# A new order for the first block of an attention and feed-forward kernel

## What is computed

```
x = x + L0_xattn(layernorm(x), ctx)   # q, k, v; 16 heads of 16; softmax over 64 keys; then relu(out @ W1 + b1) @ W2 + b2
x = x + L0_ffn(layernorm(x))          # gate: top 2 of 8 experts; relu(x @ wi + bi + lora of the expert) @ wo, gated
x = x + L1_xattn(layernorm(x), ctx)   # one head of 256, softmax over 64 keys
x = x + L1_ffn(layernorm(x))          # x @ weight.T + pooled(x) @ disha
```

## Time and profile before

| | |
|---|---|
| runs of the kernel | median 313.52 us, 313.37 to 314.22, 3 runs |
| the profiled execution | 313.58 us, span 311.6 us: 1.98 us lie around the span |
| PE busy | 296.1 us, 95% of the span |
| PEld busy | 273.4 us, 88% |
| DVE busy | 257.1 us, 83% |
| ACT busy | 172.1 us, 55% |
| POOL busy | 161.2 us, 52% |

### The profile page before, as it was taken

One profiled execution on the slowest core, in us unless ns is written; L12 is line 12 of the kernel. 1 busy time (PEld: TensorE's weight loads), 2 busy tenths in 40 slices (PEclk: granted clock), 3 DMA queues, 4 the chain that ended last, 5 costly groups with the idle time before them and its releaser, 6 DMA issues.

```text
span 311.6 us, 6575 instructions
## 1 busy us (share of the span) xinstructions
PE 296.1 (95%) x2488; PEld 273.4 (88%) x2488; DVE 257.1 (83%) x706; ACT 172.1 (55%) x359; POOL 161.2 (52%) x156
## 2 busy tenths in 40 slices
PE   6879998999999999999999999999999999999982
PEld 5749887999989998999999998999899998999971
DVE  3689878979899988998799889998899879756676
ACT  3447488675567357535846465835853584434521
POOL 2754666695085705581386308560559044803562
PEclk9799999999999999999999999999999999999996
DMA  7993230015021230133012311122023000000000
GB/s 227 394 375 110 61 78 2 0 36 135 2 17 38 68 102 2 17 96 112 2 17 69 102 37 17 44 76 87 3 27 94 34 2 0 2 23 13 0 36 34
DMA packets 15903, 20.17 MB, mean 65 GB/s; under 512 B 2912, under 2 KB 11872, under 8 KB 15616
## 3 DMA queue, kind: packets, MB, share of 16 engines
q1 hardware_dynamic: 14176, 16.18, 18.9%
q10 hardware_dynamic: 1696, 3.57, 3.2%
...
## 4 chain that ended last, share of the span: by engine, by line
PE 63%; DVE 24%; ACT 5%; POOL 3%; issue 2%; DMA 2%; SPq 0%; DVEq 0%; POOLq 0%
PE psI L338 12%; PE psI L552 12%; PE psP L347 8%; PE psI L347 4%; PE psT L338 4%; DVE st L1254 3%; ACT xn L950 3%; DVE qu_l L1288 2%; DVE mx L1296 2%; PE psP L487 2%; DMA kv<-in_kv 2%; PE psS L347 2%; PE psS L460 2%; POOL rs L1726 2%; PE psT L362 2%
## 5 line engine op out<-in xcount | busy, mean ns | idle before, releaser
L1726 POOL TENSOR_TENSOR rs<-ve,mhalf 128x2 f32<-128x2 f32 x30 | 22.0, 732 | 88.7 <-DVE ve L1265 88.7
L1749 POOL TENSOR_TENSOR hid_l<-r,hid_h 128x512 fp32r<-128x512 f32 x32 | 40.9, 1290 | 16.1 <-ACT hid_h L1029 16.1
L552 PE MATMUL psI<-at_h,lb_h 128*128 128x256 f32 x120 | 34.8, 290 | 0.8 <-DVE at_l L1378 0.8
L552 PE MATMUL psI<-at_h,lb_l 128*128 128x256 f32 x120 | 33.9, 282 | 0.0
L552 PE MATMUL psI<-at_l,lb_h 128*128 128x256 f32 x120 | 33.7, 281 | 0.0
L1386 DVE SCALAR_TENSOR_TENSOR r<-psI,nbi,r 128x256 f32<-128x256 f32 x60 | 26.1, 476 | 6.5 <-PE psI L552 6.5
L1743 POOL TENSOR_TENSOR hs_l<-hs,hs_h 128x512 fp32r<-128x512 f32 x15 | 19.6, 1312 | 20.1 <-ACT hs_h L1009 19.5
L950 ACT ACTIVATE xn<-xmid,nmr,rs 128x256 f32<-128x256 f32 x16 | 8.7, 593 | 35.6 <-POOL nmr L1730 35.6
L1024 ACT ACTIVATE r<-psI,first 128x256 f32<-128x256 f32 x60 | 25.1, 473 | 4.4 <-PE psI L552 4.4
L552 PEld LDWEIGHTS psI<-at_h,lb_h 128*128 128x128 f32 x120 | 22.6, 188 | 4.3 <-ACT r L1024 2.9
L1029 ACT ACTIVATE hid_h<-r 128x512 fp32r<-128x512 f32 x32 | 20.0, 627 | 11.2 <-DVE r L1386 11.0
...
## 6 DMA issues: line engine op xcount, KB each, us to landing
stack<-qu_h SPq DMA_DIRECT2D x56, 64.0 KB, 2.1
...
stack<-qu_l SPq DMA_DIRECT2D x28, 64.0 KB, 2.1
...
raw_wo<-in_wo SPq DMA_DIRECT2D x1, 1024.0 KB, 13.2
```

Source lines behind the costliest of these rows:

```text
L552: last = mm(bank[:, k * T:(k + 1) * T], (WH, WL)[x]["lb"][:, 0, f * P:(f + 1) * P], AT[y][:, which, :], start=False, stop=q == 2, skip_gro ...
L1726: G_.tensor_tensor(rs[:, :], ve[:, :], mhalf[:, :], ALU.pow).then_inc(S(f"ln{j}_rs"), 1)
L1749: G_.tensor_tensor(HL[:, two, :], R1[:, two, :], as32(HH[:, two, :]), ALU.subtract).then_inc(S("hidl"), 1)
```

## The change

Nothing of what is computed changes; the first block's work is put in another order, and some of it on other engines.

- x of block 0 is loaded in two halves, one from SP and one from ACT, where the second stands ahead of ACT's other loads (a1, wq, w1, w2). kv1 is loaded ahead of wi.
- values of v0 for batch 0 no longer stand between keys0 and the transposes on PE; they and query_means come after a_queries(0). query_means works on fp32r operands (4 products) in place of fp32 ones.
- first_attend issues the sums for two pairs, then the values, in banks of their own, so that the reciprocal waits for the sums alone.
- Block 1's queries are computed in three passes placed around the two halves of a_out(0); values1 and folded_keys come earlier, and the row scores of block 1 after them.
- v0 is copied by ACT (value_rows) and masked by POOL (first_values) in place of DVE; the copy of the query means goes from DVE to ACT.
- Low parts: w1 and ga go from DVE to POOL, w2 from POOL to DVE; the first half of wo moves from the end of POOL's opening into body(1), behind `gated`. The second half of the indicators moves to the end of body(2).
- fold_turn moves behind a_scores of body(1), and f_lora_transposes(0) ahead of them; lora_high(0) goes ahead of the exps on ACT.
- Fillers: 4, then 2 after keys0, 1 before a_queries(0) (before: 4, then 2 and 1 around a_queries(0)).

The core of the diff:

```diff
@@ -44,7 +44,7 @@
...
+HIGH_ORDER = ["wq", "w1", "w2", "wi0", "ga", "wi1", "lb", "wo"]
 GW = 2 * KEYS + D
...
-                sp.dma_start(x_of_block(b), x_v[b]).then_inc(S("x_in"), 16)
+                if b == 0:
+                    sp.dma_start(XINS[0][:, 0, :], x_v[0][:, 0, :]).then_inc(S("x_in"), 16)
+                else:
+                    sp.dma_start(x_of_block(b), x_v[b]).then_inc(S("x_in"), 16)
...
-            sp.wait_ge(S("x_in"), 16)
+            sp.wait_ge(S("x_in"), 32)
             load_x(1)
+            sp.dma_start(kv1[:, :], io["kv1"]).then_inc(S("ld_kv1"), 16)
             load("wi")
             load("ga")
-            sp.dma_start(kv1[:, :], io["kv1"]).then_inc(S("ld_kv1"), 16)
...
+                    parts = [(P_(0)[:, m * T:(m + 1) * T], w("wq", m * P), x_of(XTA)) for m in range(KC)]
+                    last = passes(parts, range(KC), ((x, y),), (x, y) == (0, 0), y == 1)
+                    if y:
+                        last.then_inc(S("q_ps"), 1)
...
-                        last = mm(P_(m)[rows, T:2 * T], ones_pair, EX[:, c, :], start=True, stop=True)
+                        last = mm(FIRST_SUMS[m][rows, 0:T], ones_pair, EX[:, c, :], start=True, stop=True)
                 last.then_inc(S("pv"), 1)
+                if m == 0:
+                    pe.wait_ge(S("v0_ready"), 3)
+                for c in range(m * GPC, (m + 1) * GPC):
+                    rows = slice(PW * (c % GPC), PW * (c % GPC) + PW)
+                    last = mm(FIRST_VALUES[m][rows, 0:T], v0z[:, c * PW:(c + 1) * PW], EX[:, c, :], start=True, stop=True)
+                last.then_inc(S("pv"), 1)
...
                 if b == 0 and half == 0:
-                    pe.wait_ge(S("lo_wp"), 1)
+                    pe.wait_ge(S("lo_w"), 2)
+                    pe.wait_ge(S("ln1_l"), 2)
...
+                parts = [t["wq"][:, c * D:(c + 1) * D] for t in (wh, wl) for c in range(KC)]
                 for n, part in enumerate(parts):
-                    last = mm(S_(1)[:, 0:D], avg[:, 0:1].broadcast_to([P, P]), part, start=n == 0,
+                    last = mm(P_(1)[:, T:T + D], avg_r[:, :].broadcast_to([P, P]), part, start=n == 0,
...
-                if F_:
+                if F_ and f > 0:
                     f_lora_transposes(f)
                 if f == 0:
+                    fold_turn()
                     fold_means()
...
                 first_scores_less_maxima()
                 first_attend(0)
                 first_attend(1)
-                query_means()
-                transposes(1, 1, I_(0))
-                values(T_(1)[:, 0:D], kv0, 1).then_inc(S("v0_ps"), 1)
+                values(S_(1)[:, 0:D], kv0, 1).then_inc(S("v0_ps"), 1)
                 keys1()
+                pe.wait_ge(S("rec"), 1)
+                transposes(1, 1, P_(1))
+                values1()
                 a_hidden(0, 0)
-                pe.wait_ge(S("centred"), 2)
+                pe.wait_ge(S("v0"), BATCH)
                 a_hidden(0, 1)
-                a_queries(1, I_(1))
+                a_queries(1, ((0, 0),))
                 a_out(0, 0)
+                a_queries(1, ((1, 0),))
                 a_out(0, 1)
-                pe.wait_ge(S("kt1"), 1)
-                pe.wait_ge(S("v0"), BATCH)
-                a_row_scores(1, 0, T_)
-                a_row_scores(1, 1, S_)
-                values1()
+                a_queries(1, ((0, 1),))
                 folded_keys()
+                a_row_scores(1, 0)
+                a_row_scores(1, 1, I_)
+                pe.wait_ge(S("x1"), 1)
+                transposes(2, 0, P_(1))
                 pe.wait_ge(S("mx"), 2 * NT - 1)
-                transposes(2, 0, T_(1))
+                constant_parts()
+                f_gate(0, 1)
                 pe.wait_ge(S("mx"), 2 * NT)
-                constant_parts()
+                f_base(0, 0)
+                pe.wait_ge(S("ln2_l"), 1)
                 a_max_transposes(1)
-                f_gate(0, 1)
-                pe.wait_ge(S("gb"), 1)
-                f_base(0, 0)
                 constant_row()
-                pe.wait_ge(S("v1"), 1)
                 f_base(0, 1)
-                fold_turn()
+                f_lora_transposes(0)
...
+            def value_rows(b, bank):
+                act.wait_ge(S("v0_ps"), b + 1)
+                A(v0[:, b * D:(b + 1) * D], bank[:, 0:D], ACT.Identity).then_inc(S("v0"), 1)
...
+                if f == 0:
+                    act.wait_ge(S("kd_out0"), 32)
+                    act.wait_ge(S("kd_out1"), 32)
                     lora_high(f)
-                if A_:
-                    exps(a, 1)
+                exps(a, 0)
...
+            act.dma_start(XINS[0][:, 1, :], x_v[0][:, 1, :]).then_inc(S("x_in"), 16)
...
+                normalise(1, 0, x_of_block(0))
...
-                normalise(1, 0, x_of_block(0))
                 high(1, 0, XTA, T_(1))
                 high_weights("w1")
                 queries(0)
+                act.wait_ge(S("centred"), 1)
+                value_rows(0, P_(1))
+                A(wqm[:, :], P_(1)[:, T:T + D], ACT.Identity).then_inc(S("centred"), 1)
...
                 normalise(1, 1, x_of_block(1))
+                value_rows(1, S_(1))
                 attended(0, 0)
+                high(1, 1, XTA, P_(1))
                 high_weights("wi", 0, 2)
-                high(1, 1, XTA, I_(0))
                 attended(0, 1)
+                high_weights("ga")
                 high_weights("wi", 1, 2)
...
+                high_weights("wo")
                 maxima(1)
                 sorted_exps(0)
-                high_weights("wo")
...
             def first_attended(m):
-                dve.wait_ge(S("pv"), m + 1)
-                V.reciprocal(REC[:, m, :], P_(m)[:, T:2 * T]).then_inc(S("rec"), 1)
+                dve.wait_ge(S("pv"), 2 * m + 1)
+                V.reciprocal(REC[:, m, :], FIRST_SUMS[m][:, 0:T]).then_inc(S("rec"), 1)
                 dve.wait_ge(S("rec"), m + 1)
-                V.tensor_tensor(O32[:, m, :], P_(m)[:, 0:T], REC[:, m, :], MULT).then_inc(S("o32"), 1)
+                dve.wait_ge(S("pv"), 2 * m + 2)
+                V.tensor_tensor(O32[:, m, :], FIRST_VALUES[m][:, 0:T], REC[:, m, :], MULT).then_inc(S("o32"), 1)
...
                 first_attended(0)
                 first_attended(1)
-                dve.wait_ge(S("centred"), 1)
-                V.tensor_copy(wqm[:, :], S_(1)[:, 0:D]).then_inc(S("centred"), 1)
                 attended_low(0, 1)
-                low(1, 1, XTA, I_(0))
-                first_values(1, T_(1)[:, 0:D])
+                low_weights("w2")
+                low(1, 1, XTA, P_(1))
                 keys_of_second()
+                hidden_low(0, 1)
                 low_weights("wi", 1, 2)
-                hidden_low(0, 1)
-                queries_low(1)
-                low_weights("ga")
                 first_residual(0)
                 dve.wait_ge(S("x1"), 1)
                 norm_stats(2, 0, XMID)
-                row_max(1, 0, psT)
-                row_max(1, 1)
-                low(2, 0, XTF, T_(1))
+                queries_low(1)
...
+                    if f == 0:
+                        low_weights("wo", 0, 2)
...
+                if a == 2:
+                    pool.wait_ge(S("ln3_rs"), f + 1)
+                    indicators(1)
...
+            def first_values(b):
+                at = slice(b * D, (b + 1) * D)
+                ready = 3 * b
+                pool.wait_ge(S("v0"), b + 1)
+                G_.tensor_tensor(v0[:, at], v0[:, at], vmask, ALU.mult).then_inc(S("v0_ready"), 1)
+                pool.wait_ge(S("v0_ready"), ready + 1)
+                G_.tensor_tensor(v0[:, at], v0[:, at], bvrow0, ALU.add).then_inc(S("v0_ready"), 1)
+                if b == 0:
+                    pool.wait_ge(S("v0_ready"), 2)
+                    G_.tensor_tensor(v0z[:, :], v0[:, at], vmask, ALU.mult).then_inc(S("v0_ready"), 1)
...
-                pool.wait_ge(S("ld_first"), 16)
-                pool.wait_ge(S("ln1_nmr"), 1)
-                indicators(0)
-                indicators(1)
                 pool.wait_ge(S("ld_vrows"), 16)
                 G_.tensor_copy(heads[:, :], heads32).then_inc(S("tables"), 1)
-                low_weights("w2", 0, 1)
+                low_weights("w1", 0, 1)
+                first_values(0)
+                scale(1, 1)
+                pool.wait_ge(S("ld_first"), 16)
+                pool.wait_ge(S("ln1_nmr"), 2)
+                indicators(0)
+                second_row_keys()
+                attended_low(0, 0)
+                first_values(1)
                 pool.wait_ge(S("ld_kept"), 16)
                 residual(0)
-                scale(1, 1)
-                attended_low(0, 0)
-                pool.wait_ge(S("kt0_h"), KC)
-                second_row_keys()
+                low_weights("ga", 0, 1)
                 hidden_low(0, 0)
                 low_weights("wi", 0, 2)
```

142 lines of the change are left out of this document (63 added, 79 removed).

## The result

The changed kernel takes 317.61 us (median, 315.93 to 319.41) against 313.42 for the kernel before on the same chip; the ratio is 1.0138, 95% interval 1.0117 to 1.0159. The medians differ by 4.2 us, and the ratio stands for 4.3; 0.996 was forecast. The profiled execution took 318.99 us with a span of 316.0.

What follows compares the result with a forecast made beforehand. PE bounds the blocks behind the opening, so only the start of f_first counts: 0.2 us from xmid and 1.1 from the end make it 1.3 earlier, 313.58 to 312.3, median 312.2 us; range 310.5 to 314.5.

Steps and rivals of the forecast that it cites:

- Row scores of block 0: First stage of the opening: row scores start at 13.15 in place of 15.08, 1.9 us earlier, bounds 1.6 to 2.4.
- w1's landing: First stage: w1, behind half of x in ACT's queue, lands at 11.2 and sets w_h, qu_h and the row scores.
- The end part: From xmid to f_first: at_l no longer waits for gate, held by POOL's wo_l; 1.1 us gained.
- just in time: Block 1's query copies by SP: the stack DMAs land at 45.2, ahead of a_scores at 45.9.
- Rival (c): Ahead of xmid: POOL becomes the bound; 0.9 us slower, 314.5, if its wi_l starts later than 33.9; chance 0.15.
- (d): End of body(2): the moved indicators product ks holds up DVE; at most 2.81 us, about 1.4 net, 313.6; chance 0.04.
- The step that failed: Opening, on POOL: w_l of w1 (2.35 us) and three small v products end by about 16.8; values wanted at 19.
- The second failing step: First block's softmax chain: same instructions with PE at full clock ahead of it, so exps end 1.9 us earlier.
- Rival (b): Hole ahead of xn's transposes: PE's clock halves, f_first at 49.6, 0.4 later than before, 313.5 us; chance 0.25.
- The pivot: At xmid: POOL's wi_l goes before DVE's, so xmid comes at 35.05, 1.85 us behind x1_ps; PE hole 2.9 us.
- Rival (a): At xmid: DVE takes wi_l right behind hs_l, xmid at 33.2, f_first 1.8 us earlier, 311.6 us; chance 0.22.

Runs made afterwards that it cites:

- kb_wi: The changed kernel with POOL's w_l of w1 behind DVE's kd_l and POOL's half of wi_l behind DVE's half, no filler added; ratio 0.9943 to the kernel before.
- before_wo: The kernel before with only POOL's first half of wo_l moved from the end of its opening into body(1), behind gated; ratio 0.9936, median of all executions 313.98 us.
- warm: The changed kernel with six fillers on PE behind the first block's row scores; ratio 1.0054 to the kernel before.
- kb_free: The changed kernel with POOL's w_l of w1 made to wait until DVE's kd_l is done; ratio 1.0044 to the kernel before.
- kb_first: The changed kernel with DVE's kb ahead of xta_l, as in the kernel before, and nothing else; ratio 1.0061 to the kernel before.
- before_kv0: The kernel before with only batch 0's values of v0 moved behind the first block's queries, in their own bank, and fillers rearranged; 312.91 us, ratio 0.9975.
- kv0_wo: The kernel before with batch 0's values of v0 behind the first block's queries and wo_l's first half behind gated; 312.93 us, ratio 0.9988.
- best4: The changed kernel with POOL's w_l of w1 behind DVE's kd_l, POOL's wi_l half behind DVE's, four fillers behind the first row scores; 311.24 us, ratio 0.9901.

## Why the prediction was wrong

**The gains.** Row scores of block 0 were forecast at 13.15. In kb_wi they begin at 13.17 and the exps at 18.16, 1.9 earlier than before: this term was right in size, once DVE is free of POOL, though that is one execution against one, and the row scores of the kernel before stand at 15.08 in its profile and at 16.80 in before_wo's. Not right was its working, and the match is luck. x did land earlier (norm_stats at 3.70, not 4.60), but the half of x in ACT's queue put wq back (wq_h at 7.16, not 5.60 as before), so that xn, ready at 6.15, stood behind wq_h; w1's landing, which the prediction took for the limit, did not matter: in kb_wi w_h ran at 9.83, right behind xta_h, and the row scores came straight behind PE's own query_means (12.53 to 13.17), which the sum had as hidden. The end part was forecast at 1.1 and is worth 0.4 (xmid to f_first 13.53) to 1.0 (12.99 in warm). gate waits for nothing, as forecast (0.16 us at 51.86); but in the changed kernel a_scores of block 1 waits 0.42 us for the last stack DMA, which was "just in time" in the sum. Rival (c) did not happen: POOL's hs_l waited 1.79 us for ACT's hs_h, and its wi_l came directly behind it, so POOL was not the bound, though this product started at 36.03, past the 33.9 from which (c) has the kernel slower: it came late behind hs_h. Nor did (d): with ks in the body of block 2, f_first to the end is 262.2 us against 262.4.

**The step that failed** is in the part up to the first row scores: "POOL has w_l of w1 (2.35 ...) and three small v products ahead of the first values". It costed this product for POOL and for who waits for POOL, and not for DVE. The rule was known: in the next part the same text lets the engines get into each other's way, and counts 0.5 us there. But DVE's kb, 1.21 us with two SBUF inputs, was moved behind xta_l, a part of the diff that neither the list of changes nor the prediction names, and so it stood exactly where w_l starts. The price was 2.22 us up to the maxima.

**The second failing step** is "The softmax chain behind them (maxima, exps) is the same instruction for instruction, so the exps end 1.9 us earlier as well", with "PE at full clock, since two fillers now lie in the hole between keys and transposes" ahead of it. The instructions were the same, and row scores to exps took 6.53 us in place of 5.00. The fillers do lie there, and the clock was 1.00 there. But the kernel before had its half clock at 9.8 to 13.2 and was at 1.00 through the softmax; the changed one entered the softmax chain with a hole of 1.20 and then of 1.63 us and fell to 0.50 for the 10 us in which PE is the limit. Rival (b) looked for this only in the hole ahead of xn's transposes. The length of the hole does not decide it alone: with 0.85 us the clock fell in kb_wi and kb_free, with 0.86 it did not in the kernel before.

Measured against kb_wi and the kernels at full clock, the changed kernel's f_first is late by: 2.22 (kb and kd_l); 0.68 (maxima to exps: 3.87 from the start of the second maximum to the exps, 3.19 in kb_wi, whose clock fell only afterwards); 2.26 (exps to a_hidden, 10.11 against 7.84 or 7.85 in five kernels with the same instructions at 1.00); 1.88 (a_hidden to xmid, 9.07 against 7.19, POOL's wi_l); 0.41 (xmid to f_first, 13.53 against 13.12). That is 7.45 us, of which the change's own gains pay 2.9, and 4.5 remain. 4.1 are turns at the ports, 2.9 the clock, and 0.4 the wait for the stack DMA. The 2.9 gained are against the profiled execution of the kernel before, which had its half clock and a late kv0.

**The pivot** was right in kind and partly in place. The prediction gave it 1.85 us at DVE's wi_l; kb_first shows it there, the changed kernel on hs_l one instruction earlier, for 1.62 us of PE. With PE held there, the hole ahead of the transposes was 1.16 us in the changed kernel and not 2.9. Which of the two it is hangs on a lead of 0.1 to 0.3 us. Rival (a), the other order of turns, did not come about in any run without an added wait.

**What stays open** is why the clock falls in one execution and not in another of the same instructions. And the kernel before itself runs from 311.0 to 318.2 us over all occasions. One part of that is likely kv0's landing, which moves its first transposes (9.58 us in its profile, 11.06 in before_wo, which has the same instructions there), as the smaller spread of before_kv0 and kv0_wo suggests. A gain of 1 us is measured against that spread, and best4's 1% is a gain in the median: its six executions took 310.4 to 311.6 us, and the fastest of the kernel before, over all occasions, 311.0 to 311.5. That the hole ahead of the maxima brings the clock down was shown by filling it, never by widening it.
